# State-space loop on one core: GpSimd multiplies one head of four of the first group's state as well, and additions, outputs and their signals go by group, second group first

## The reference

```python
def step(h_state, ins):
    x_t, dt_t, B_t, C_t = ins
    a = jnp.exp(dt_t[:, :, None, None] * A[None])
    h_state = a * h_state + B_t[:, None, None, :] * x_t[..., None]
    y_t = jnp.einsum('bhdn,bn->bhd', h_state, C_t)
    return (h_state, y_t)
...
_, ys = jax.lax.scan(step, h0, xs)
```

## Time and profile before

| what | value |
|---|---|
| median of 3 executions | 1594.03 us (1591.66 to 1597.79) |
| the profiled execution's own time | 1593.92 us |
| its span, first to last instruction | 1592.2 us |
| the state-space loop in it, first increment to last output | about 785 to 1247 us |
| mean granted TensorE clock | 0.979 |

### The profile page before, as it was taken

The page is one execution under the profiler, slowest core; times in us unless marked ns, Lnnn a source line. Parts: engine busy times, 40 slices in busy tenths (PEclk is TensorE's granted clock), DMA queues, the critical chain, the costliest instruction groups (busy, mean ns, idle before and its releaser), DMA issues. The chain is left out here.

```text
span 1592.2 us, 33554 instructions
## 1 busy us (share of the span) xinstructions
PE 1359.0 (85%) x12662; PEld 1021.3 (64%) x12662; DVE 1344.2 (84%) x1703; ACT 1053.1 (66%) x2455; POOL 986.2 (62%) x828
## 2 busy tenths in 40 slices
PE   4899999999999999979677667677676899999992
PEld 4688888888888888765233333333333688888881
DVE  3899999999999999987599999999999635666662
ACT  3656666666666666535599899899899234555550
POOL 1778888788888878656166666666666341323323
PEclk9999999999999999999799999999999999999996
DMA  4511111111111111007454110200000016888872
GB/s 120 191 36 43 43 36 46 40 43 43 43 43 36 49 37 30 1 2 153 129 97 63 22 24 1 38 9 1 1 1 1 1 62 267 304 310 310 305 269 86
DMA packets 104155, 132.87 MB, mean 83 GB/s; under 512 B 39514, under 2 KB 95265, under 8 KB 100552
## 3 DMA queue, kind: packets, MB, share of 16 engines
q1 hardware_dynamic: 94696, 62.99, 16.1%
q0 software_dynamic: 9312, 67.90, 12.0%
HBM read 110.44 MB, written 14.45 MB: 78 GB/s over the span
## 5 line engine op out<-in xcount | busy, mean ns | idle before, releaser
L564 POOL TENSOR_TENSOR half<-prob 128x512 f32<-128x512 f32 (+1 forms) x208 | 266.7, 1282 | 108.5 <-ACT prob L600 106.9
L596 ACT ACTIVATE prob<-ps_s,mx 128x64 f32<-128x64 f32 (+1 forms) x624 | 151.5, 322 | 236.3 <-DVE prob L709 236.3
L1359 DVE TENSOR_TENSOR state<-ps_u,state 128x1024 f32<-128x1024 f32 x252 | 296.7, 1219 | 4.3
L704 DVE TENSOR_REDUCE mx<-ps_s 128x16 f32<-128x1024 f32 (+1 forms) x208 | 253.2, 1217 | 14.9 <-PE ps_s L637 11.2
L1318 PE MATMUL ps_y<-state,cz 128*32 128x256 f32 x2048 | 247.5, 384 | 2.1 <-DVE state L1359 1.1
L637 PE MATMUL ps_s<-qbd,kT 64*128 64x256 f32 (+1 forms) x1664 | 217.4, 396 | 23.0 <-ACT prob L596 17.5
L1245 ACT ACTIVATE ps_a<-A,dt 128x256 f32<-128x256 f32 x504 | 210.4, 463 | 35.1 <-DVE state L1354 35.1
L709 DVE TENSOR_TENSOR prob<-ps_s,mx 128x832 f32<-128x832 f32 (+1 forms) x208 | 213.0, 1024 | 7.1
L1229 POOL TENSOR_TENSOR state<-direct,state 128x1024 f32<-128x1024 f32 x64 | 151.6, 2369 | 84.3 <-PE ps_y L1318 84.2
L1300 PE MATMUL ps_u<-x_rows,b_diag 48*128 48x256 bf16 x1024 | 78.1, 272 | 138.2 <-DVE state L1359 134.8
L637 PEld LDWEIGHTS ps_s<-qbd,kT 64*128 64x128 f32 (+1 forms) x1664 | 151.0, 184 | 67.2 <-issue 35.9
(11 more groups left out here) (260 smaller groups left out, 3116.8 us busy)
## 6 DMA issues: line engine op xcount, KB each, us to landing
raw<-in_ctxT_dram SPq DMA_DIRECT2D x80, 268.0 KB, 2.8
x_rows<-ssm_x SPq DMA_DIRECT2D x96, 64.0 KB
raw<-in_ctxT_dram SPq DMA_DIRECT2D x16, 261.0 KB, 2.8
b_diag<-zeros SPq DMA_DIRECT2D x2, 2048.0 KB, 9.0
x_slots<-zeros SPq DMA_DIRECT2D x1, 3456.0 KB, 14.1
xg<-x_slots SPq DMA_DIRECT2D x27, 128.0 KB, 6.5
y_slots<-y SPq DMA_DIRECT2D x27, 128.0 KB, 4.5
ssm_x<-xp SPq DMA_DIRECT2D x6, 384.0 KB, 3.9
```

The costliest lines, as they stand in the source:

```text
L564: pool.tensor_tensor(half[0:rows, :, :], prob[0:rows, g % SLOTS, :, 0:L // 2], prob[0:rows, g % SLOTS, :, L // 2:L], ALU.add).then_inc(hal ...
L704: nc.vector.tensor_reduce(mx[0:rows, g % 2, :], part, AX_X, ALU.max, negate=True)\
L1359: nc.vector.tensor_tensor(h, flat(ps_u[k % 2][:, :, :]), h, ALU.add).then_inc(state_ready, 1)
```

## The change

Two things change together, all of it inside `state_space`.

1. VectorE multiplies only the first 192 columns (OWN, three heads) of each block of group 0's state. GpSimd multiplies the fourth head (4 x 64 columns), with a decay that ScalarE writes into a new SBUF tile, `shared_decay`. ScalarE's decays of group 0 are signalled in two parts.
2. TensorE's increments and outputs are issued group by group, group 1 first: four matmuls of group 1's increment, four of its output, four of group 0's increment, four of its output. Each has its own wait and its own signal. `y_added` counts two for a pair. VectorE adds to group 1 first.

```diff
@@ GpSimd @@
-                pool.wait_ge(y_added, n + 1)
+                pool.wait_ge(y_added, 2 * n + 1)
                 pool.tensor_tensor(h, flat(direct[t % 2][:, hh, :, :]), h, ALU.mult).then_inc(pool_kept, 1)
+                part = state[:, 0, hh, :, OWN:HALF]
+                pool.wait_ge(decay_ready, 2 * n + 1)
+                pool.wait_ge(y_added, 2 * n + 2)
+                pool.tensor_tensor(part, shared_decay[:, hh, :, :], part, ALU.mult).then_inc(pool_kept, 1)
...
@@ ScalarE, decay @@
+                if n >= 2:
+                    act.wait_ge(pool_kept, 2 * n - 2)
+                piece(shared_decay[:, hh, :, :], t, 0, NH // 2 * hh + NH // 2 - 1).then_inc(decay_ready, 1)
                 if n:
                     act.wait_ge(kept, n)
-                pieces(ps_a[:, :, :], t, 0, hh).then_inc(decay_ready, 1)
+                for c in range(0, OWN, HD):
+                    ins = piece(ps_a[:, :, c:c + HD], t, 0, NH // 2 * hh + c // HD)
+                ins.then_inc(decay_ready, 1)
...
@@ TensorE, inputs @@
                 if pair:
-                    pe.wait_ge(state_ready, 2 * pair)
+                    pe.wait_ge(state_ready, 2 * pair - g)
                 for n in range(NHI):
-                    for g in range(2):
-                        ins = nc.tensor.matmul(ps_u[g][:, n, :], m["b_diag"][rows_of(g), ch % 2, NHI * tt + n, :],
-                                               m["x_rows"][rows_of(g), ch % 2, tt, HALF * hh:HALF * (hh + 1)],
-                                               start=True, stop=True, skip_group_check=True)
-                        if n == NHI - 1:
-                            ins.then_inc(u_ready, 1)
...
+                    ins = nc.tensor.matmul(ps_u[g][:, n, :], m["b_diag"][rows_of(g), ch % 2, NHI * tt + n, :],
+                                           m["x_rows"][rows_of(g), ch % 2, tt, HALF * hh:HALF * (hh + 1)],
+                                           start=True, stop=True, skip_group_check=True)
+                ins.then_inc(u_ready, 1)
...
@@ TensorE, outputs @@
-                pe.wait_ge(state_ready, 2 * pair + 2)
+                pe.wait_ge(state_ready, 2 * pair + 2 - g)
...
+                col = 32 * ((quad + 2 * g) % 4)
                 for n in range(NHI):
-                    for g in range(2):
-                        col = 32 * ((quad + 2 * g) % 4)
-                        c0 = CZ * tm + 32 * (NHI * g + n)
-                        ins = nc.tensor.matmul(ps_y[g][col:col + 32, HALF * hh:HALF * (hh + 1)],
...
+                    c0 = CZ * tm + 32 * (NHI * g + n)
+                    ins = nc.tensor.matmul(ps_y[g][col:col + 32, HALF * hh:HALF * (hh + 1)],
...
             for pair in range(PAIRS + 1):
-                if pair < PAIRS:
-                    inputs(pair)
-                if pair:
-                    outputs(pair - 1)
+                for g in (1, 0):
+                    if pair < PAIRS:
+                        inputs(pair, g)
+                    if pair:
+                        outputs(pair - 1, g)
+                if pair and pair % (2 * TB) == 0:
+                    skips(pair // (2 * TB) - 1)
...
@@ VectorE @@
+                    own = state[:, 0, hh, :, 0:OWN]
+                    dve.wait_ge(decay_ready, 2 * n + 2)
+                    dve.wait_ge(y_added, 2 * n + 2)
+                    nc.vector.tensor_tensor(own, ps_a[:, :, 0:OWN], own, ALU.mult).then_inc(kept, 1)
+                for g in (1, 0):
+                    h = flat(state[:, g, hh, :, :])
+                    dve.wait_ge(u_ready, 2 * pair + 2 - g)
+                    if t:
+                        if g == 0:
+                            dve.wait_ge(kept, n + 1)
+                        dve.wait_ge(pool_kept, 2 * n + 2 - g)
+                        nc.vector.tensor_tensor(h, flat(ps_u[g][:, :, :]), h, ALU.add).then_inc(state_ready, 1)
```

More of the change, by code:

```diff
@@ L1190, in state_space @@
         block = ctx.enter_context(nc.Block())
-        def at(k):
-            return k // 4, k % 4 // 2, k % 2
         def flat(v):
@@ L1201, in number @@
             return 2 * (t - 1) + hh
+        OWN = HALF - HD
         @block.sync
@@ L1284, in _, with inputs @@
         def _(pe):
-            def inputs(pair):
+            def inputs(pair, g):
                 t, hh = pair // 2, pair % 2
                 ch, tt = t // TB, t % TB
[L1288 to L1295, removed]
+                if g:
+                    if t == FIRST and hh == 0:
+                        pe.wait_ge(b_loaded[0], 16 * B_LOADS)
+                    if tt == 0 and hh == 0:
+                        if ch:
+                            pe.wait_ge(b_loaded[ch], 16 * (B_LOADS + (ch == 1)))
+                        pe.wait_ge(x_loaded[ch % 2], 16 * ROW_LOADS * (ch + 1))
+                    if t == TB // 2 and hh == 0:
+                        pe.wait_ge(x_loaded[2], 16 * ROW_LOADS)
@@ L1306, in outputs @@
-            def outputs(pair):
+                    ins = nc.tensor.matmul(ps_u[g][:, n, :], m["b_diag"][rows_of(g), ch % 2, NHI * tt + n, :],
+                                           m["x_rows"][rows_of(g), ch % 2, tt, HALF * hh:HALF * (hh + 1)],
+                                           start=True, stop=True, skip_group_check=True)
+                ins.then_inc(u_ready, 1)
+            def outputs(pair, g):
                 t, hh = pair // 2, pair % 2
                 ch, tt, quad, tm = t // TB, t % TB, t // 4, t % 4
-                pe.wait_ge(state_ready, 2 * pair + 2)
[L1310 to L1313, removed]
-                for n in range(NHI):
-                    for g in range(2):
-                        col = 32 * ((quad + 2 * g) % 4)
-                        c0 = CZ * tm + 32 * (NHI * g + n)
-                        ins = nc.tensor.matmul(ps_y[g][col:col + 32, HALF * hh:HALF * (hh + 1)],
-                                               m["cz"][:, quad % 2, c0:c0 + 32], state[:, g, hh, n, :],
-                                               start=(tm == 0 and hh == 0 and n == 0), stop=False, skip_group_check=True)
-                ins.then_inc(y_added, 1)
[L1322 to L1327, removed]
@@ new lines, in outputs, with skips @@
+                for n in range(NHI):
+                    c0 = CZ * tm + 32 * (NHI * g + n)
+                    ins = nc.tensor.matmul(ps_y[g][col:col + 32, HALF * hh:HALF * (hh + 1)],
+                                           m["cz"][:, quad % 2, c0:c0 + 32], state[:, g, hh, n, :],
+                                           start=(tm == 0 and hh == 0 and n == 0), stop=False, skip_group_check=True)
+                ins.then_inc(y_added, 1)
+            def skips(ch):
+                for g in range(2):
+                    for c in range(XC):
+                        ins = nc.tensor.matmul(ps_y[g][:, c * P:(c + 1) * P], m["xs"][:, c, tokens_of(2 * ch + g)],
+                                               m["skip"][:, c, :], start=False, stop=True, skip_group_check=True)
+                    ins.then_inc(y_full, 1)
@@ L1344, in sum_squares @@
                 nc.vector.tensor_reduce(m["ss"][:, g:g + 1], square[:, :], AX_X, ALU.add).then_inc(summed, 1)
-            for k in range(STEPS):
-                t, hh, g = at(k)
-                h = flat(state[:, g, hh, :, :])
+            for pair in range(PAIRS):
+                t, hh = pair // 2, pair % 2
+                n = number(t, hh)
                 if t:
[L1350 to L1355, removed]
-                    else:
[L1357 to L1363, removed]
+                    own = state[:, 0, hh, :, 0:OWN]
[10 more added lines that the diff above has]
+                        nc.vector.tensor_tensor(h, flat(ps_u[g][:, :, :]), h, ALU.add).then_inc(state_ready, 1)
+                    else:
+                        nc.vector.tensor_copy(h, flat(ps_u[g][:, :, :])).then_inc(state_ready, 1)
+                if t and t % TB == 0 and hh == 0:
                     for i in range(2):
                         take_output(2 * (t // TB - 1) + i)
-                if t > TB and t % TB == 1 and g == 1:
+                if t > TB and t % TB == 1:
                     sum_squares(2 * (t // TB - 1) + hh)
```

25 lines of the change are left out of this document (15 added, 10 removed).

## The result

| what | before | changed |
|---|---|---|
| median, four executions each | 1594.89 us | 1750.28 us (1747.40 to 1753.04) |
| ratio | 1 | 1.0975 (95% interval 1.0946 to 1.1003) |
| span of the profiled execution | 1592.2 us | 1745.7 us |

The account below looks back on a forecast made before the run. VectorE bound the loop before; after the change TensorE would, at 4.78 us a pair. Pairs +148.1, skip terms +6.9, end +3.1 and start +2 gave +160.1 us on 1593.9: 1754 us, range 1735 to 1790.

Parts of the forecast that it names:

- The step that decided it: TensorE's outputs: two groups share the array today; a group's block alone would take as many steps as both groups' block.
- The rival that TensorE stays hidden: State-space loop: TensorE needs about 2.4 us a pair, VectorE or ScalarE bounds at 3.25 us; 1553 us, chance 0.05.
- One reading in the prediction: List of waits before the change: the prediction said that VectorE has no row at all.
- The block of 2.39 us: TensorE, one group's increments (0.54 us) plus outputs (1.85 us), needed twice a pair: 4.78 us.
- The price of a switch from outputs to increments: TensorE between blocks: no row showed it at full clock without a skip term between; taken as within 2.39 us a block.
- neither bound (4.42 and 5.06): Us a pair on TensorE: free, overlapping switches 4.42 (1708 us, chance 0.06); full drain 5.06 (1790 us, chance 0.1).
- pairs 2 to 127, with skip terms: Loop: 125 pairs at 4.78 us, +148.1 us, and three skip terms no longer hidden, +6.9 us.
- the end: Last increments to last skip term: 4.78 us plus two blocks of outputs, 3.70, is 8.48 against 5.37: +3.1 us.
- the start: Loop start: group 1's outputs alone at low clock, most of group 0's at full; pair 2 about 794 against 792.12: +2 us.
- That nothing else bounds the pair: Pair of 4.78 us: VectorE, GpSimd and ScalarE all have over 1 us to spare.
- That the share is worth nothing: GpSimd's part of group 0's product: the 0.3 us a pair it saves VectorE lands in a wait for TensorE.

Follow-up runs that it names:

- the kernel with two tiles for a group: Changed kernel, but the odd ones of a group's four output matmuls go to a neighbouring column tile (computation changed): 1551.38 us, ratio 0.9732 to the kernel before.
- the second kernel above: Changed kernel without GpSimd's share (VectorE multiplies all four heads of group 0), order by group kept: 1748.41 us, ratio 1.0959 to the kernel before.
- the kernel with adjacent blocks: Changed kernel with its blocks reordered: increments of group 1, of group 0, then outputs of group 1, of group 0: 1618.87 us, ratio 1.0158 to the kernel before.

## Why the prediction was right

**The step that decided it** was that two groups' matmuls run side by side only because they take turns in the queue, read from 16 records in 1.92 us against a step of 0.216 us. The profile after shows 8 records in 1.91 us, and the kernel with two tiles for a group shows that neither waits nor switches, but the tile, makes the difference. The rival that TensorE stays hidden would have given 1553 us; the kernel with two tiles took 1551.38, with 3.23 us a pair over the loop against 3.60 before (increments of pair 2 at 792.25, of pair 127 at 1196.20). So its price was right, and its condition did not hold.

One reading in the prediction is too strong: of VectorE there is a row in the list of waits before, the 1.2 us shown above. It bears on no term of the sum.

**The block of 2.39 us** for each group, 4.78 a pair, measured 2.39 and 4.77. VectorE's and GpSimd's times within the pair, laid out in the prediction, came within 0.2 us: with group 1's increments at 1003.09, the product starts 0.17 us later, GpSimd's share ends after 0.94, and the addition of group 0 starts after 3.03. The price of a switch from outputs to increments, the one unseen, is that of the switch into the skip term; neither bound (4.42 and 5.06) was met.

**The terms of the sum**, by the starts of the first increments of a pair:

| term | forecast | measured |
|---|---|---|
| pairs 2 to 127, with skip terms | 604.4 us for 449.4: +155.0 | 602.9: +153.5 |
| the end | 8.48 us for 5.37: +3.1 | 6.55: +1.2 |
| the start | +2 | 6.68 us for 7.09: -0.4 |

The first increments also begin 0.7 us earlier (784.31 against 785.03), which makes 153.6, the difference of the spans being 153.5. The end was mis-sized, and the start came out otherwise in this execution. Of the end I wrote that it would be "4.78 plus two blocks of outputs"; but there no increments stand between the blocks:

```profile
1393.91 0.61 PE L1308 MATMUL ps_u<-x_rows,b_diag 48*128 48x256 bf16 x4
1396.29 0.61 PE L1308 MATMUL ps_u<-x_rows,b_diag 48*128 48x256 bf16 x4
1396.83 3.70 PE L1325 MATMUL ps_y<-state,cz 128*32 128x256 f32 x24
1400.46 2.05 PE L1333 MATMUL ps_y<-skip,xs 128*128 128x128 f32 x16
```

Twenty-four records of three blocks, of group 0, 1 and 0, take 3.70 us, where one behind another they would take 5.3 (23 steps of 0.216 and 0.38). That a block overlaps the one before it, where both are outputs of different tiles, was missing in the term. Of the start I wrote that "the first outputs run at the low clock". They did not in this execution:

```profile
784.31 0.62 PE L1308 MATMUL ps_u<-x_rows,b_diag 48*128 48x256 bf16 x8 [0.94 <-PEq L864]
786.23 0.61 PE L1308 MATMUL ps_u<-x_rows,b_diag 48*128 48x256 bf16 x4 [1.29 <-DVE state L1374]
786.76 1.91 PE L1325 MATMUL ps_y<-state,cz 128*32 128x256 f32 x8
...
790.99 0.61 PE L1308 MATMUL ps_u<-x_rows,b_diag 48*128 48x256 bf16 x4
```

The eight records take 1.91 us, the pace of the rest of the loop, and the granted clock is 1.00. The execution of the second kernel above, with the same order on TensorE, did have the low clock:

```profile
788.46 3.47 PE L1318 MATMUL ps_y<-state,cz 128*32 128x256 f32 x8
792.40 1.91 PE L1318 MATMUL ps_y<-state,cz 128*32 128x256 f32 x8
794.25 0.61 PE L1301 MATMUL ps_u<-x_rows,b_diag 48*128 48x256 bf16 x4
...
core 0: us, PE busy (x), PEclk, DMA share, GB/s
788.00:792.00 4.00, 4.00 (x14) 0.57 0.20 12
```

It goes as the prediction describes it: group 1's outputs alone at the low clock, group 0's at the full one, and pair 2 at 794.25. From its first increments (785.91) to there it is 8.34 us, 1.7 more than in the changed kernel's profile and 1.25 more than before. So the low clock at the start does not come from TensorE's order as such; what decides it is open. The term of +2 described one of these executions and not the other, and how near it comes is luck. The changed kernel's profiled execution is the fastest of its four; how the other three began is not on record.

**That nothing else bounds the pair** held: VectorE's product (0.96 us, forecast 0.9) and GpSimd's (0.73, forecast 0.735) both have time to spare. That the share is worth nothing beside TensorE's 4.77 us is shown by its removal.

## What to carry to other kernels

Before matmuls are reordered so that a signal can go out earlier, look for rows in which n records take less than n steps of their own size: those matmuls share the array, and they do so because a near neighbour in the queue has another tile. In this kernel a finer order on TensorE cost nothing where each finer block still held two tiles, and where its extra time fell into a wait (the increments by group); splitting a block by its moving columns (here the channels) provided the second tile. And a unit that takes work from the bound (GpSimd here) gains only when the round trip through it has room: the same share was worth 0 us in one order and 30 us in the other.

## What the runs showed of the hardware

- Blocks of outputs of different tiles that follow each other without alternating overlap in part. In both places looked at (the end of the changed kernel's loop, and the kernel with adjacent blocks) a block's first record starts beside the fifth of the eight before it: 24 records in three blocks took 3.70 us, 16 in two took 2.81. In the stretch ahead of the second block's start in the changed kernel, five records have begun:

```profile
1396.80:1397.72 0.92, 0.89 (x5) 0.47 (x6) 1.00 0.00 0
```

  Two adjacent blocks of four increments overlap whole, if the second has nothing to wait for: eight records in 0.62 us at the start of the changed kernel's loop (784.31) and in the kernel with adjacent blocks (791.78), as long as four. In all four places the second block starts beside the fourth-last record of the one before it. What sets this distance was not tried.
- Halving the moving size did not cost pace: with two tiles, sixteen records of 128 moving columns took as long (1.07 us) as eight of 256 (1.06 us), although each needs its own weight load, recorded at 0.11 us.
- A float32 matmul in a tile of 32 columns has the same step as in the full array, 0.216 us for 256 moving columns a record (eight records in 1.91 us, against six in 1.46 us in the earlier trace rows).
